# Mixture of experts: rows carry a tag of place and weight, results are scattered by GpSimd, the last part loads plain tiles

## What is computed

```
x = _rmsnorm(src + sa, norm1_w)                  # S = 4096 tokens, D = 256
shared = _swiglu(flat @ W_shared_in) @ W_shared_out
...                                              # 8 experts in 2 groups; softmax in the chosen group
topv, topi = jax.lax.top_k(p_expert, TOPK)       # TOPK = 2
w = zeros((S, E)).at[arange(S)[:, None], topi].set(topv)
h = _swiglu(flat @ W1_shared)                    # 512 wide, the same for all experts
for e in range(E):
    routed = routed + h @ W2_experts[e] * w[:, e:e + 1]
out = _rmsnorm(x + shared + routed, norm2_w)     # and the outer residual is added
```

## Time and profile before

| | us |
|---|---|
| runs timed | 5840.5, 5853.87, 5853.37 (median 5853.37) |
| profiled execution, its own time | 5842.88 |
| span of its trace, first to last instruction | 5841.0 |
| pairs (from the trace) | 5174 to 5574 |
| slots and woven chunks | 5574 to 5777 |
| drain | 5777 to 5841 |

### The profile page before, as it was taken

How to read it: one execution, slowest core, us unless ns; L and a number is a source line. 1 busy time by engine, 2 the same in 40 slices (tenths; PEclk the granted TensorE clock), 3 DMA queues, 4 the chain that set the end, 5 groups by cost and what they waited for, 6 DMA issues and landing times. The chain is left out here.

```text
span 5841.0 us, 139849 instructions
## 1 busy us (share of the span) xinstructions
PE 5046.9 (86%) x53868; PEld 3300.4 (57%) x53868; DVE 3899.8 (67%) x6903; ACT 3137.2 (54%) x4732; POOL 2462.5 (42%) x2096
## 2 busy tenths in 40 slices
PE   7688888888799789788989989997889999989985
PEld 3455555555487544377777778885532333346674
DVE  5899999999797855544444434443688888844424
ACT  5899999999654845422222223333445666642222
POOL 1778777788575623344444431112530000002104
PEclk9899999999999999889999999998889999999997
DMA  5202020020111233423333331112652222232256
GB/s 169 50 17 53 13 49 21 24 38 13 38 45 38 67 125 151 168 96 104 108 101 108 105 106 51 55 44 53 163 149 42 46 45 45 42 96 77 72 157 188
DMA packets 441107, 457.16 MB, mean 78 GB/s; under 512 B 227874, under 2 KB 376729, under 8 KB 432273
## 3 DMA queue, kind: packets, MB, share of 16 engines
q1 hardware_dynamic: 418704, 397.99, 24.2%
q0 software_dynamic: 8192, 25.17, 1.3%
q10 hardware_dynamic: 13568, 25.17, 1.2%
HBM read 276.38 MB, written 171.82 MB: 77 GB/s over the span
## 5 line engine op out<-in xcount | busy, mean ns | idle before, releaser
L538 POOL TENSOR_SCALAR attn_u<-attn_rel,attn_aux 128x1024 f32<-128x1024 f32 x512 | 1090.4, 2130 | 271.8 <-DVE attn_nm L565 271.7
L689 PE MATMUL attn_tp<-attn_ident,attn_pr 128*128 128x128 f32 x4096 | 574.1, 284 | 241.0 <-ACT attn_pt L628 238.9
L3366 DVE TENSOR_REDUCE attn_mx<-attn_mp 128x1 f32<-128x512 f32 x1024 | 652.7, 685 | 90.2 <-PE attn_mp L3445 89.2
L689 PEld LDWEIGHTS attn_tp<-attn_ident,attn_pr 128*128 128x128 f32 x4096 | 450.7, 143 | 461.6 <-ACT attn_pt L628 322.1
L557 DVE SCALAR_TENSOR_TENSOR attn_u<-attn_rel,attn_aux,attn_u 128x1024 f32<-128x1024 f32 x512 | 681.1, 1331 | 27.5 <-POOL attn_u L538 18.9
L3430 ACT ACTIVATE attn_pt<-attn_st 128x1024 f32<-128x1024 f32 x512 | 506.7, 1023 | 281.4 <-PE attn_st L3456 280.5
L649 ACT ACTIVATE attn_pr<-attn_pr,attn_nm 128x1024 f32<-128x1024 f32 x512 | 604.9, 1181 | 87.9 <-DVE attn_nm L565 87.6
L565 DVE CUSTOM_DVE_ANT_0 attn_pr<-attn_u,attn_s 128x1024 f32<-128x1024 f32 x512 | 619.0, 1209 | 48.0 <-PE attn_s L680 35.1
L628 ACT ACTIVATE attn_pt<-attn_tp 128x512 f32<-128x512 f32 x1024 | 568.6, 626 | 10.7 <-issue 5.6
L3445 PE MATMUL attn_mp<-attn_kt,attn_qt 96*128 96x512 bf16 x1024 | 371.8, 394 | 16.1 <-DMA attn_qt<-s_q 15.2
L680 PE MATMUL attn_s<-attn_kt,attn_qt 96*128 96x512 bf16 x1024 | 317.4, 393 | 52.5 <-DVE attn_nm L565 24.5
(11 more groups left out here) (549 smaller groups left out, 10709.0 us busy)
## 6 DMA issues: line engine op xcount, KB each, us to landing
s_qkv<-gin_qkv SPq DMA_DIRECT2D x32, 1536.0 KB
core_qk<-s_qkv SPq DMA_DIRECT2D x32, 1024.0 KB, 5.1
attn_qt<-s_q SPq DMA_DIRECT2D x384, 64.0 KB, 3.0
attn_kt<-s_k SPq DMA_DIRECT2D x192, 128.0 KB, 4.3
moe_rows<-s_hid_s SPq DMA_DIRECT2D x78, 256.0 KB
core_arow<-s_alr SPq DMA_DIRECT2D x32, 512.0 KB
core_grow<-s_gar SPq DMA_DIRECT2D x32, 512.0 KB, 3.7
core_vv<-s_qkv SPq DMA_DIRECT2D x32, 512.0 KB, 3.6
```

Of the source, the lines that this page charges most:

```text
L538: pool.tensor_scalar(u[:, x % 4], rel[:, z % 2, 1], aux[:, s, 4 + NH + h:5 + NH + h], aux[:, s, 4 + 2 * NH + h:5 + 2 * NH + h], ALU.mult, ...
L689: ins = pe.transpose(tp[k][:, n], pr[:, x % BUF, (4 * k + n) * P:(4 * k + n + 1) * P], ident[:])
L3366: dve.reduce_max(mx[w % 2][:].rearrange("p h t a -> p (h t a)")[:, j:j + 1], bank(("row", number))[:], AX.X).then_inc(m["max_done"], 1)
```

## The change

The tag of a row is two numbers, a place and a weight. Its place is the row in which its result shall stand in a new scratch `y_t`, which is in the order of the tokens: k x 4096 + token for the k-th choice. The places are constants, loaded once into `tag`; the weight, formerly `wsel`, is written beside them. In the part on pairs GpSimd scatters the tag (8 bytes for each row) to `tag_s` right behind each scatter of hidden rows, with the same indices. Where SP writes zeros behind a region it also writes tags from `spare`, whose places lie behind the 8192 real rows.

In the part on slots `load_rows` also loads the slot's 128 tags, from the third row of `table`; that load waits until the result of four slots earlier is copied, since it reuses its buffer. VectorE converts the place to an index (`home`) and multiplies the result with the weight while it copies it. GpSimd scatters the result to `y_t`; SP stores nothing. In the part on chunks SP loads two plain tiles for each chunk (`load_results`, two buffers), and VectorE adds them in two operations over the pair. `gather`, `gidx` and the six operations that made it are gone.

```
             def pad(h):
...
                     sp.dma_start(d["hid_s"][bass.ds(row, P), :], zero[:]).then_inc(m["pad_out"], 16)
+                    sp.dma_start(d["tag_s"][bass.ds(row, P), :], spare[:, h, n]).then_inc(m["pad_out"], 16)
             def load_rows(s):
...
                 need(sp, "tb_mm", s - 3)
                 row = sp.value_load(table[0:1, h, 1, s % SL:s % SL + 1], min_val=0, max_val=2 * SORTED - P)
                 sp.dma_start(rows[:, s % 4], d["hid_s"][bass.ds(row, P), :]).then_inc(e["row_in"][s % 4], 16)
-            def store_rows(s):
-                h, at_ = s // SL, s % SL * P
-                sp.wait_ge(m["y_copy"], s + 1)
-                sp.dma_start(d[f"y_s{h}"][at_:at_ + P, :], yb[:, s % 3]).then_inc(e["y_out"][s % 3], 16)
+                need(sp, "y_copy", s - 3)
+                row = sp.value_load(table[0:1, h, 2, s % SL:s % SL + 1], min_val=0, max_val=2 * SORTED - P)
+                sp.dma_start(tags[:, s % 4], d["tag_s"][bass.ds(row, P), :]).then_inc(e["row_in"][s % 4], 16)
+            def load_results(c):
+                h = c // HALF
+                if c % HALF == 0:
+                    for n in range(3):
+                        sp.wait_ge(e["y_out"][n], 16 * (h + 1) * SL // 3)
+                need(sp, "acc2", c - 1)
+                for k in range(TOPK):
+                    at_ = k * T + c * 2 * P
+                    sp.dma_start(g[:, c % 2, k], d["y_t"][at_:at_ + 2 * P, :].rearrange("(z p) c -> p z c", p=P)).then_inc(e["g_in"][c % 2], 16)
...
+            sp.dma_start(tag[:], d["moe_tag"]).then_inc(m["tag_in"], 16)
+            sp.dma_start(spare[:], d["moe_spare"]).then_inc(m["tag_in"], 16)
+            sp.wait_ge(m["tag_in"], 32)
...
             for h in range(2):
...
+                sp.dma_start(d["tag_s"][at_:at_ + 7 * P, :].rearrange("(n p) c -> p n c", p=P), spare[:, h, NE:]).then_inc(m["zero_out"], 16)
...
-                if s >= 1:
-                    store_rows(s - 1)
                 if tail(s) and tail(s)[1] == 0:
+                    load_results(tail(s)[0])
                     load_x5(tail(s)[0])
-            store_rows(LAST - 1)
+            for c in range(HALF, HALF + 2):
+                load_x5(c)
             for c in range(HALF, PAIRS):
-                load_x5(c)
+                load_results(c)
+                if c >= HALF + 2:
+                    load_x5(c)
...
                         pool.indirect_dma_start(d["hid_s"], bass.IndirectOffsetOnAxis(idx[:, t, k:k + 1], 0), hid[:, t % 4], None
                                                 ).then_inc(e["sc_out"][t % 4], 16)
+                        pool.indirect_dma_start(d["tag_s"], bass.IndirectOffsetOnAxis(idx[:, t, k:k + 1], 0), tag[:, t, k], None
+                                                ).then_inc(e["tag_out"][t % 2], 16)
+            def results(s):
+                pool.wait_ge(m["home_done"], s + 1)
+                pool.wait_ge(m["y_copy"], s + 1)
+                pool.indirect_dma_start(d["y_t"], bass.IndirectOffsetOnAxis(home[:, s % 3], 0), yb[:, s % 3], None).then_inc(e["y_out"][s % 3], 16)
...
             def copy_out(s):
-                dve.wait_ge(m["ob_mm"], s + 1)
+                dve.wait_ge(e["row_in"][s % 4], 32 * (s // 4) + 32)
                 if s >= 3:
                     dve.wait_ge(e["y_out"][s % 3], 16 * (s // 3))
-                dve.tensor_copy(yb[:, s % 3], ub[s % 2][:, 0:D]).then_inc(m["y_copy"], 1)
+                dve.tensor_copy(home[:, s % 3], tags[:, s % 4, 0:1]).then_inc(m["home_done"], 1)
+                dve.wait_ge(m["ob_mm"], s + 1)
+                dve.tensor_scalar(yb[:, s % 3], ub[s % 2][:, 0:D], tags[:, s % 4, 1:2], None, ALU.mult).then_inc(m["y_copy"], 1)
             def gathered(c):
...
+                both = acc[:, 2 * c:2 * c + 2]
+                dve.tensor_tensor(both, both, g[:, c % 2, 0], ALU.add).then_inc(m["acc1"], 1)
+                dve.wait_ge(m["acc1"], c + 1)
+                dve.tensor_tensor(both, both, g[:, c % 2, 1], ALU.add).then_inc(m["acc2"], 1)
```

More of the change, by code:

```diff
@@ L3551, in stage_moe @@
         pick, posn, posf = r.sb("pick", [P, 2, TOPK, NE]), r.sb("posn", [P, 2, NE]), r.sb("posf", [P, TILES, TOPK])
-        fe, shift, moved = r.sb("fe", [P, NE]), r.sb("shift", [P, HT * TOPK, NE]), r.sb("moved", [P, HT * TOPK])
-        idx, gidx = [r.sb(n, [P, TILES, TOPK], mybir.dt.uint32) for n in ("idx", "gidx")]
-        wsel = r.sb("wsel", [P, TILES, TOPK])
+        idx = r.sb("idx", [P, TILES, TOPK], mybir.dt.uint32)
+        tag, spare, tags = r.sb("tag", [P, TILES, TOPK, 2]), r.sb("spare", [P, 2, NE + 7, 2]), r.sb("tags", [P, 4, 2])
+        home = r.sb("home", [P, 3, 1], mybir.dt.uint32)
         cnt, num, cumi = r.sb("cnt", [P, NE]), r.sb("num", [P, NE]), r.sb("cumi", [P, NE])
@@ L3719, in _ @@
                     scatter(i)
-            for h in range(2):
-                for n in range(3):
-                    pool.wait_ge(e["y_out"][n], 16 * (h + 1) * SL // 3)
-                pool.wait_ge(m["gidx_done"], h + 1)
-                for c in range(h * HALF, h * HALF + HALF):
-                    gather(c)
-                    if c > h * HALF:
-                        last_root(c - 1)
-                last_root(h * HALF + HALF - 1)
+            for s in range(LAST):
+                results(s)
+                if tail(s) and tail(s)[1] == 2:
+                    last_root(tail(s)[0])
+            for c in range(HALF, PAIRS):
+                last_root(c)
         @block.vector
@@ L4182, in layout @@
     out["moe_off"] = np.repeat(region[:, None], 2, axis=1).astype(np.float32)
+    tag = np.zeros((P, TILES, 2, 2), np.float32)
+    tag[..., 0] = np.arange(P)[:, None, None] + P * np.arange(TILES)[None, :, None] + T * np.arange(2)[None, None, :]
+    out["moe_tag"] = tag
+    spare = np.zeros((P, 2, 15, 2), np.float32)
+    spare[..., 0] = 2 * T + np.arange(P)[:, None, None] + P * np.arange(30).reshape(1, 2, 15)
+    out["moe_spare"] = spare
     out["moe_slot"] = np.arange(SLOTS, dtype=np.float32)
```

55 lines of the change are left out of this document (19 added, 36 removed).

## The result

The changed kernel takes 5865.14 us in the median of 17 runs, the kernel before 5845.63 in 17 runs on the same chip: ratio 1.0035, 95% interval 1.0025 to 1.0045. It is slower by some 20 us, where I had forecast 5842 and no change that a measurement could tell. The forecast was a change of -11.0, counted from the median of three runs, which was 7.7 us above that of all 17; the change that came is +20. The profiled execution has a span of 5862.9 us against 5841.0.

What follows compares the result with a forecast made beforehand. TensorE was taken to bound pairs and slots, waits between engines the woven stretch, GpSimd's gathers the drain. Terms 0 + 4.8 + 4.1 - 1.6 - 18.3 = -11.0, counted from the runs' median, gave 5842 us; range 5832 to 5853.

Steps and rivals of the forecast that it cites:

- The woven stretch: Slot 43 to the last copy: 10.8 us a group against 10.56, +2.0, less 3.6 given back at the begin: -1.6.
- Slots 6 to 42: Slots before the results are loaded: SP at 2.28 us a slot becomes the bound over TensorE's 2.17, +4.1.
- rival 4: Slots: tags landing after 6.3 us make TensorE wait, +40 in all, 5893; begins at a landing of 3.5; chance 0.13.
- Pads: Between slots 4 and 5: tag writes beside SP's zeros and later tags delay TensorE 3.9 us, slot 7 0.9: +4.8.
- Drain: Last copy to the end: plain result loads replace gathers, 3.8 us a chunk, 45.4 against 63.7: -18.3.
- Start and pairs: Start and pairs: pair 2's loads about 8 us later but hidden, 64 more GpSimd DMAs fit: 0, up to +4.
- rival 2: Slots, woven stretch, drain: address reads partly overlap issue, SP takes 2.1 or less a slot; 5833 against the median; chance 0.22.
- rival 3: Woven stretch and drain: results land after 5 us under load, +10 and +5.6; +5 in all, 5858; chance 0.13.

Runs made afterwards that it cites:

- full: Changed kernel with one address read a slot, eight tag buffers, pad writes by ScalarE, four result, x5 and output buffers, constants' wait in pair 4: ratio 0.9951.
- before_scatter: The kernel before with the change's 64 small scatters added to the pairs, from a constant, which nobody reads: ratio to before 1.0001.
- addr_tags8: The changed kernel with one address read a slot for both loads and eight tag buffers instead of four: ratio to the kernel before 1.001.
- one_address: The changed kernel with SP reading one address a slot and issuing both loads from it: ratio to the kernel before 1.0014.
- addr_tags8_pads: The changed kernel with one address read a slot, eight tag buffers, and the second half's zeros and tags written by ScalarE's queue: ratio to before 0.9973.

## Why the prediction was wrong, point by point

Of the 27.3 us between the forecast of the stage (-11.0) and what it took (+16.3) the woven stretch has 14.0, start and pairs 4.1, the slots 3.2, the drain 3.1 and the pads 2.9.

**The woven stretch, -1.6 predicted, +12.4 measured: the step that failed.** I took SP's work (10.5 a group) and the loops (7.1 + L for the results, 5.6 + L for the tags) apart, and let the longest decide. They aren't apart. The tag load stands in SP's one queue, behind the results' loads, and is released only by the copy of slot s-4, so SP can't run ahead when it has time. "It must fit in 4 x 2.28 = 9.1, so it is hidden as long as L is below 3.5" holds for a steady L; it leaves out that SP then keeps a smaller lead: 1.1 slots not yet begun between slots 45 and 76, where it had 1.7. Late landings, and the loads of results in the same queue, then become stalls of TensorE. In place of my 10.8 a group took 12.64. Take either lock away and part of it goes (11.40, 11.99); take both and it costs 10.66, and 10.79 between slots 48 and 72, where I had read the 10.56 of before: the number that I had forecast. The 3.6 that I gave back for a smoother begin was right in kind: it was 5.2 here, and all changed kernels begin in 6.5 to 7.4. But before and its variants begin in anything from 6.5 to 12.7, so its size hangs on which execution of before was profiled, and in the table it hides part of the failure: eight groups alone are +17.6, where I had +2.0.

**Slots 6 to 42, +4.1 predicted, +7.3 measured.** The sign was right and the reason only half. SP's price of an address is confirmed: 1.11 to 1.14 each, 2.67 for a slot with one more. But a slot costs SP 2.22 and not 2.28, against TensorE's 2.17, which is 1.8 over 35 slots: with eight buffers 6 to 41 took 77.6, which is 35 times 2.22, with SP's two address reads still there. The other 5.5 are the tags' wait. This is my rival 4 by its place, and not by its price: the tags land after 2.4, not 6.3, and it began below the point that I gave for it.

**Pads, +4.8 predicted, +7.7 measured.** Right in kind. Mis-sized were the second write of a pad (0.78 instead of 0.49, in all +2.3) and the landing of the tags behind them (4.6 instead of 2.2). Together they are 4.7, more than the 2.9 that is missing; the 0.9 for slot 7 did not come, since TensorE turned it without a wait, and the last 0.9 I can't place.

**Drain, -18.3 predicted, -15.2 measured.** First addition, chunk and the reason for 3.8 a chunk (buffers of `x5` and the results) were right, and full shows it by removing them. What is missing is the end: from the last addition to the end of the span I took 9.7 from before, and it is 12.4 to 12.5 in every profile of the changed kernel and its variants, and 11.3 in before_scatter. The last norm's addition starts as long after the last chunk's additions as before, and SP is done some 6 us before the end. What runs there is GpSimd's DRAIN: 6.54 us before and in its variants, 8.09 in before_scatter, 9.24 after and in every variant of it, and the other engines' last instructions follow its end. The stage's indirect DMAs are 128, 192 and 206 in these kernels, so the DRAIN is longer where GpSimd has issued more of them, though not in proportion; why, no run shows.

**Start and pairs, 0 predicted, +4.1 measured.** I had pair 2's loads 8 late and still hidden; they were issued about 9 late relative to the stage, the last one landed after 7.4 instead of 2.4, behind the matrices' loads, and TensorE waited 2.0. That is 2 to 2.5 of the 4.1. The rest is the clock in the same pair: it took 26.8 at a granted clock of 0.94, where before it took 23.0 at 1.00; the other pairs are alike. Why some executions have pairs of 25.6 to 27.3 stays open: it isn't the scatters alone, and it isn't the late writes alone. In some of them, as in addr_tags8, TensorE waits 2.5 for VectorE's counts in a pair where it is 1.6 in before, and the pair takes 23.9 at the full clock.

**SP keeps up** (rival 2) was wrong in the slots. **Results land late** (rival 3): they landed after 3.9 in the median, near my 3.7, and in the woven stretch VectorE waited for them 7.9 us in five waits, of which the group shown above has none.

## What to carry to other kernels

A load that a loop adds costs its issuer's time first; where its address comes from a register this was 1.1 us, for 1 KB as for 256 KB, and one read that serves two loads, or a queue with idle time, gives much of it back. A new load in an in-order queue also brings its buffer's wait into that queue: count how many steps the queue is ahead afterwards, and give the smallest tile as many buffers as the others need for their lead, since eight bytes a row take next to no room. When two estimates, an engine's work and a loop through it, lie as close as 10.5 and 10.8, add up what each lateness does rather than take the larger.

## What was not expected of the hardware

Indirect scatters land unevenly: 2.4 to 6.8 us in the trace after, with late ones at about every eighth slot in one_address (slots 10, 18, 26, 34) and addr_tags8_pads (10, 18, 26, 33), where the traces give no cause. In five of the eight groups after, the load of rows behind the three loads of results and `x5` is issued 1.5 to 1.8 after the last of them, where the address read explains 0.8; in one_address, with the same three loads ahead, it is 0.8 in seven of eight, so the burst alone isn't the cause. The pairs show TensorE's two clock levels, 2.4 and 1.2 GHz, as steps of time for the same work: 22.9 at a granted clock of 1.00 on average, 24.6 at 0.93, and 27.3 at 0.875, with 1.0 more of waiting. And the DRAIN of GpSimd's queue at the end of the program took 6.54 to 9.24 us, the same within 0.01 in every profile of kernels with the same indirect DMAs.
